# A gap of 192 bytes in front of the split rows: their start in SBUF against that of the split weights

## What is computed

```python
xn = layernorm(x)
agg = segment_sum((xn @ W_gnn)[src] * edge_weight[:, None], dst)
x = x + relu(agg) + linear_attention(xn)
h = layernorm(x)
for _ in range(30):
    h = h + 0.01 * tanh(h)
    h = h * sigmoid(h)
    h = layernorm(h) * ln_w + ln_b
    h = h @ W.T + b
out = x + h
```

## The kernel before, in words

| tile | before | after | before, mod 512 | after, mod 512 |
|---|---|---|---|---|
| w_high, w_low | 48736, 50784 | the same | 96, 96 | 96, 96 |
| v_high0, v_high1 | 200352, 204448 | 200544, 204640 | 160, 160 | 352, 352 |
| v_low0, v_low1 | 208544, 212640 | 208736, 212832 | 160, 160 | 352, 352 |

## Time and profile before

### The profile page before, as it was taken

One profiled execution on the slowest core, in us unless ns is written; L12 is line 12 of the kernel. 1 busy time (PEld: TensorE's weight loads), 2 busy tenths in 40 slices (PEclk: granted clock), 3 DMA queues, 4 the chain that ended last, 5 costly groups with the idle time before them and its releaser, 6 DMA issues.

```text
span 4121.0 us, 83954 instructions
## 1 busy us (share of the span) xinstructions
PE 3907.4 (95%) x29240; PEld 3676.3 (89%) x29240; DVE 3765.0 (91%) x7281; ACT 3428.6 (83%) x5103; POOL 3225.0 (78%) x3853
## 2 busy tenths in 40 slices
PE   0899989999999999999999999999999999999999
PEld 0788878989898999999999999999999999899999
DVE  6888778989989999999999999999999999999998
ACT  3333278888888999999899999989999999999998
POOL 4777788888888888888888888888888886555555
PEclk8999999999999999999999999999999999999999
DMA  8555322222223222222322222233222221100000
GB/s 303 166 157 152 112 82 79 78 78 80 77 79 98 82 80 76 79 80 80 100 80 80 77 80 83 75 92 92 76 79 82 75 80 54 52 1 1 1 2 26
DMA packets 215405, 340.39 MB, mean 83 GB/s; under 512 B 79160, under 2 KB 152502, under 8 KB 214994
## 3 DMA queue, kind: packets, MB, share of 16 engines
q0 software_dynamic: 80768, 219.99, 18.6%
q1 hardware_dynamic: 120126, 83.28, 6.9%
q10 hardware_dynamic: 14100, 31.75, 2.3%
HBM read 298.20 MB, written 36.65 MB: 81 GB/s over the span
## 4 chain that ended last, share of the span: by engine, by line
PE 51%; DVE 31%; ACT 9%; POOL 5%; issue 3%; DMA 1%; ACTq 0%; DVEq 0%; SPq 0%; POOLq 0%
PE MM L1432 26%; PE TR L1424 11%; PE AGG L1340 9%; DVE st L1154 7%; DVE v_low L1194 6%; DVE T L1179 6%; ACT T L753 3%; DVE hot L1062 3%; POOL gat_even L557 2%; PE XB L1352 2%; ACT v_high L767 2%; ACT T L758 2%; DVE ve L1159 2%; POOL rs L531 1%; DVE k_n L1094 1%
## 5 line engine op out<-in xcount | busy, mean ns | idle before, releaser
L557 POOL DMA_INDIRECT gat_even<-xn_d,src_cur x1496 | 1500.2, 1003 | 396.3 <-issue 350.4
L1432 PE MATMUL MM<-w_high,v_high 128*128 128x256 f32 x5880 | 1706.1, 290 | 0.0
L1432 PE MATMUL MM<-w_high,v_low 128*128 128x256 f32 x5880 | 1643.2, 279 | 0.0
L1432 PE MATMUL MM<-w_low,v_high 128*128 128x256 f32 x5880 | 1643.0, 279 | 0.0
L1432 PEld LDWEIGHTS MM<-w_low,v_high 128*128 128x128 f32 x5880 | 1113.9, 189 | 0.0
L1432 PEld LDWEIGHTS MM<-w_high,v_high 128*128 128x128 f32 x5880 | 1109.6, 189 | 0.0
L1432 PEld LDWEIGHTS MM<-w_high,v_low 128*128 128x128 f32 x5880 | 1106.9, 188 | 0.0
L1154 DVE BATCH_NORM_STATS2 st<-T 128x6 f32<-128x512 f32 x1470 | 968.9, 700 | 131.3 <-ACT T L753 119.1
L758 ACT ACTIVATE T<-T,sh,rs 128x256 f32<-128x256 f32 x2042 | 1078.5, 592 | 4.1 <-DVE sh L1164 4.1
L767 ACT ACTIVATE v_high<-TR 128x1024 fp32r<-128x1024 f32 (+1 forms) x750 | 757.9, 1011 | 214.2 <-PE TR L1424 203.7
L1194 DVE SCALAR_TENSOR_TENSOR v_low<-TR,v_high 128x1024 fp32r<-128x1024 f32 (+1 forms) x750 | 896.3, 1195 | 26.3 <-ACT v_high L767 25.3
(11 more groups left out here) (189 smaller groups left out, 2662.3 us busy)
## 6 DMA issues: line engine op xcount, KB each, us to landing
gat_even<-xn_d,src_cur POOLq DMA_INDIRECT x1496, 2.8
a_x<-in_x SPq DMA_DIRECT2D x24, 512.0 KB, 7.3
xn_d<-a_x ACTq DMA_DIRECT2D x24, 512.0 KB, 5.9
out_rows<-x_cur SPq DMA_DIRECT2D x23, 512.0 KB
a_x<-xn_d ACTq DMA_DIRECT2D x20, 512.0 KB, 3.9
x_n<-xn_d SPq DMA_DIRECT2D x80, 128.0 KB, 2.3
x_d<-x SPq DMA_DIRECT2D x80, 128.0 KB
x_cur<-x_d SPq DMA_DIRECT2D x20, 512.0 KB, 3.8
```

What stands on the lines that cost most here:

```text
L557: pool.indirect_dma_start(gat[gathered_in(j)][c][:], None, xn_d, bass.IndirectOffsetOnAxis(ap=src_cur[j % 2][:, c:c + 1], axis=0)).then_in ...
L1432: last = mm(MM[b][0:R, t // 2, t % 2 * D:(t % 2 + 1) * D], rows_, w, start=k == 0, stop=k == len(products) - 1)
```

## The change

One tile is named in front of the last group of tiles. It has 48 elements of 4 bytes in each partition and no instruction reads or writes it. What is named behind it moves up by 192 bytes. On each of the five engines the instructions, their order and their waits are those of before.

```diff
         z_rs = sb("z_rs", [128, 2])
 
 
+        sb("gap_split", [128, 48])
         kept = ExitStack()
         a_x += [kept.enter_context(nc.sbuf_tensor(f"a_x{b}", [128, A_DEEP, D], F32)) for b in range(A_RING - A_KEPT, A_RING)]
         kept.close()
```

## The result

The changed kernel takes 4142.67 us (median of 6 runs, 4141.33 to 4145.31) and the kernel before 4126.78 us (6 runs, 4122.69 to 4128.98). The ratio is 1.0041, with a 95% interval from 1.0031 to 1.0051. The gap makes the kernel 16 us slower.

What follows compares the result with a forecast made beforehand. PE, busy 95%, was taken to lead, L1432's matmuls holding 35.4% of the chain from 550 to 3550 us. Three address effects (DMA landing, DVE/ACT passes, matmul offset) summed to 0, giving 4127 us; range 4080 to 4160 us.

Steps and rivals of the forecast that it cites:

- third part of the sum: The 17,640 split matmuls, whose offset goes from 64 to 256; taken as without effect, 0 us.
- No effect: Likeliest case: the offset of the split matmuls changes nothing, time stays 4127 us; chance 0.40.
- comparison (b): The float32r projection at offset 320 takes 116.3 ns per 256 columns, the same as the mean at offset 64.
- Comparison (a): Float32 matmuls at offsets 64, 0 and 288 take 216, 216 and 215 ns: no offset effect, but at half the reading rate.
- Comparison (c): Projection loads fill a quarter of streaming, L1432's half, with equal loss per column; so most loss belongs to the streamed read.
- The rival on the other side: The new offset makes L1432's split matmuls slower, 4143 us if all slow, 4190 us at a third level; chance 0.26.
- slow lock: Units of split matmuls held at the slow pace, 117.7 ns; sign: mean 281 ns, no piece of 2.74 us left.
- every unit slow: All middle-stage units at 117.7 ns: 19 us more of PE, 12 to 19 us lost, 4139 to 4146 us; chance 0.15.
- third level: Split matmuls at 121.8 ns: 78 us more of PE, 51 to 78 us lost, 4178 to 4205 us; chance 0.08.
- The lock at the start: Last-round units, each starting PE after a short wait, were said to show that the start decides the pace, untouched by the change.
- share of the chain, 0.65: Middle-stage split matmuls: 1062 of 1645 us in the chain; 0.65 charged per PE us saved, 0.65 to 1 per us lost.
- marks by which a new level was to be known: In L1432: a least or median matmul time outside 276 to 281 ns, or a load longer than 187 to 192 ns.

Runs made afterwards that it cites:

- off320: Kernel before with a gap of 256 bytes in front of the split rows, offset 320 modulo 512: 4127.68 us, ratio 1.0001.
- both_moved: Kernel before with split weights and split rows both starting 192 bytes later modulo 512, offset still 64: 4126.25 us against 4126.26, ratio 1.000.
- one_more: Kernel before with the first matmul of each unit done twice, offset 64, result unchanged: ratio 1.0104, 44 us.
- weights_moved: Kernel before with only the split weights moved, to 416 modulo 512, so that the offset is 256: 4146.77 us, ratio 1.0048.
- off208: Kernel before with a gap and the split rows starting 16 bytes inside their tiles, offset 208 modulo 256: ratio 1.0006.

## Why the prediction was wrong

**The step that failed** is the third part of the sum, "No effect", and in it comparison (b). I read the projection's offset of 320 as another offset than 64 and its 116.3 ns as evidence that offsets do not matter. With a period of 256 bytes it is the same offset, as off320 shows (1.0001), so the comparison compared a thing with itself. The rows of before held no float32r matmul at any other offset.

**Comparison (a)**, float32 at offsets 0, 64 and 288, was read rightly and does not carry over. In the changed kernel the graph's sums, at an offset of 0, still take 0.86 us for 4. At some 216 ns for 256 columns nothing is lost; at 116 ns the offset costs 3.6. I had named the half rate as the weak point and then let the row count all the same.

**Comparison (c)** was overdrawn. The loss per column in the projection does not shrink with the smaller share of loading, but one row at one offset cannot say that most of the loss belongs to the streamed read alone. The argument also took a load's time from its columns, a quarter and a half of the streaming. The trace has a load under way for 188 ns in the median in both places, against distances of 233 ns in the projection and 116 ns in L1432. It left the offset too little.

**The rival on the other side** was right in kind, and had 0.26. It named "the slow lock or a new level", by load and stream asking for the same place modulo 256. A new level it is: 120.0 ns, between the 117.7 of "every unit slow" and the 121.8 of the "third level". The mean rose by 3.6 ns; 5.5 were reckoned for the third level and 1.4 for all slow. Its reason was half right. Equal places are bad, but 160 is as bad, so that equality is not all of the mechanism.

**The lock at the start.** Against an effect of the offset I also held that the last round shows the start of a unit to decide its pace. In the trace of before 5 of the 143 units behind 3551 us are fast. In both_moved, with the same offset and the same waits in the program, 100 of 143 are, so the short wait in front of a unit does not fix its pace.

**The size** was then off through the share on the path. 3.6 ns more are 46 us of PE in the loop stage; at 0.65 to 1 that is 30 to 46 us, and 18 were lost, 0.39. The 31 us less of idle time before the transposes' loads are about the rest. I took the share of the chain, 0.65, for the price of an added us. For one_more, 74 us, it is about that; in the placements it was 0.4 to 0.6. I read this from the shorter waits: a unit that waits for v_low starts no later when the one before it ends later. No run tests that reading. The measured 4142.67 us lies inside the range from 4080 to 4160 us only because that reached to such cases. That it also lies in the 4139 to 4146 us of "every unit slow" is luck: the pace rose by 3.6 ns and not by 1.4, and an added us cost 0.39 and not 0.65 to 1.

**What held.** The last round has room for a slower pace: 650.7 us against 650.1. The passes of DVE and ACT keep 1219 and 1026 ns, and the DMA its 7.2 us. Of the marks by which a new level was to be known, the median time outside of 276 to 281 ns is there (283 ns), and loads take longer in the median (192 ns for 188). The least time of 278 ns is inside, and the 330 ns belong to the moment of lower clock.

**The rule of the Trainium skill** that the load takes nothing from the running matmul ("TensorE: Matmul & The Clock Gate", "Step-by-step: what each phase is for") is not borne out for these matmuls. In weights_moved the same instructions on the same data run at 119.7 ns in place of 116.0 for the operands' places alone.

**Open.** Why the period is 256 bytes, why 64 and 192 to 224 are the good places, which of the reads meet, what sets the pace that a unit keeps, and why one_more cost more per us than the placements.

## What to carry to other kernels

In this kernel, whose float32r matmuls follow each other closely and each have a load of their own, the places of the loaded and the streamed tiles modulo 256 bytes are worth up to 3% of the pace (116.0 to 119.9 ns). A tile of a few bytes added between the two changes it; one ahead of both moves both. Whether other kernels show the same was not tried. After any change of the SBUF layout compare the distance from start to start within a unit before explaining a small difference in time by anything else. And before a row of another stage is used as evidence that a place does not matter, ask under which period the two places would be the same.

## What the runs showed of the hardware

- In the kernel before and in the changed one a unit settles to one of three paces. Over the last 12 distances of each unit, in the kernel before 459 of 718 units keep 117.8 ns and 259 keep 113.3 ns; in the changed one 714 of 718 keep 120.0 ns, while the means of whole units there go from 119.3 to 119.9 ns. At other offsets there are levels between (116.6 to 117.0 ns for whole units of off208).
- The share of fast units is not the same in two traces with one offset. With weights and rows moved together 379 of 718 units are fast, with the offset and the time of the kernel before. As each kernel has one trace, it is open whether this is the placement or differs from one execution to the next.
- At an offset of 0 or 256 the slower matmuls come with slower loads, 192 ns in the median against 188. At 160, which is as slow (119.9 ns), they do not:

```profile
L1432 PEld LDWEIGHTS MM<-w_low,v_high x5880: 187/188/331, 662.2 to 4246.1; 128*128 128x128 f32 x196
```
